# Fetching the edges of 128 work items by one indirect read of 1 KB rows, in the counting stage of a graph network kernel

## The reference, cut to what matters

```
# block 1, three times
h   = x * out_norm[:, None]
agg = segment_sum(h[src], dst, 12500) * in_norm[:, None]
x   = elu(agg @ W + b)
# then x = layernorm(x_in + x)
# block 2, once
msg = relu(x[src] + edge_attr @ W_edge.T + b_edge)
h   = x + segment_sum(msg, dst, 12500)
out = layernorm(x + relu(batchnorm(h @ W1.T + b1)) @ W2.T + b2)
```

## Time and profile before

| | |
|---|---|
| runs | 5515.8, 5519.86, 5517.15 us, median 5517.15 |
| profiled execution | 5517.41 us, its span 5515.5 us |
| counting stage in the span | 0 to about 1724 us |
| busy over the span | PE 91%, DVE 79%, POOL 72%, PE weight loads 56%, ACT 43% |
| `item_edges` gathers | 472, 663.7 us busy, mean 1406 ns |

### The profile page before, as it was taken

The page is one execution under the profiler, slowest core; times in us unless marked ns, Lnnn a source line. Parts: engine busy times, 40 slices in busy tenths (PEclk is TensorE's granted clock), DMA queues, the critical chain, the costliest instruction groups (busy, mean ns, idle before and its releaser), DMA issues.

```text
span 5515.5 us, 115543 instructions
## 1 busy us (share of the span) xinstructions
PE 5016.6 (91%) x41545; PEld 3092.8 (56%) x41546; DVE 4375.9 (79%) x14463; ACT 2369.5 (43%) x4260; POOL 3994.8 (72%) x3849
## 2 busy tenths in 40 slices
PE   7999999999878999999999999888888888887887
PEld 5566666667665555555555544455555555554555
DVE  8899988889897656666556632599999999988997
ACT  4888788887742000000000111244444444444444
POOL 6578877778861777777777777777777777777772
PEclk9999999999998999999999999999999999999997
DMA  5533344433323788888998988522222222222221
GB/s 216 192 128 125 110 151 143 152 135 133 114 81 134 275 283 288 265 289 279 275 280 269 286 296 294 177 47 46 47 45 46 43 45 45 44 44 44 45 46 38
DMA packets 463902, 826.70 MB, mean 150 GB/s; under 512 B 187235, under 2 KB 296049, under 8 KB 456625
## 3 DMA queue, kind: packets, MB, share of 16 engines
q1 hardware_dynamic: 330814, 718.16, 38.3%
q0 software_dynamic: 117952, 75.42, 7.0%
q10 hardware_dynamic: 14562, 25.66, 1.7%
HBM read 616.70 MB, written 202.14 MB: 148 GB/s over the span
## 4 chain that ended last, share of the span: by engine, by line
PE 47%; DVE 26%; POOL 13%; issue 8%; ACT 5%; DMA 1%; POOLq 0%; DVEq 0%; SPq 0%; ACTq 0%
PE banks L2574 22%; DVE tmp L1993 7%; PE banks L2486 7%; POOL rows_f L1299 5%; POOL sorted_recs L1264 5%; PE banks L2449 5%; ACT wide L2211 3%; DVE onehot L1980 3%; PE banks L2735 2%; DVE rows_f L2000 2%; DVE rows_f L1965 2%; PE banks L2456 2%; DVE rows_f L1972 2%; POOL sorted_recs L1209 2%; DVE rows_f L1639 2%
## 5 line engine op out<-in xcount | busy, mean ns | idle before, releaser
L1299 POOL DMA_INDIRECT rows_f<-table,src_key x1465 | 1416.7, 967 | 463.9 <-issue 439.4
L1264 POOL DMA_INDIRECT sorted_recs<-onehot,rows x1280 | 1236.5, 966 | 471.0 <-issue 379.2
L2211 ACT ACTIVATE wide<-banks 128x784 fp8e4<-128x784 f32 x1563 | 1208.4, 826 | 317.2 <-PE banks L2486 312.2
L2574 PE MATMUL banks<-wide,rows_f 128*128 128x512 fp8e4 (+1 forms) x4900 | 1120.0, 375 | 9.8 <-DMA wide<-counts 9.6
L1167 POOL DMA_INDIRECT onehot<-edge_runs_dram,rows_f x472 | 663.7, 1406 | 270.7 <-issue 135.4
L2449 PE MATMUL banks<-wide,onehot 128*128 128x392 fp8e4 x3125 | 783.8, 331 | 0.3 <-ACT wide L2211 0.3
L1993 DVE TENSOR_SCALAR tmp<-iota_win,rows 128x512 f16<-128x512 f16 x2450 | 750.7, 376 | 0.0
L2486 PE MATMUL banks<-rows_f 128*128 128x196 f16 (+2 forms) x5011 | 672.6, 257 | 81.9 <-DVE rows_f L1644 44.9
L2486 PEld LDWEIGHTS banks<-rows_f 128*128 128x128 f16 x5011 | 479.5, 152 | 318.3 <-ACT wide L2211 220.5
L2574 PEld LDWEIGHTS banks<-wide,rows_f 128*128 128x128 f16 x4900 | 441.0, 98 | 386.9 <-issue 9.2
L2735 PE MATMUL banks<-tmp,rows_f 128*128 128x512 f16 x2450 | 591.3, 382 | 14.6 <-DVE rows_f L2000 14.6
(11 more groups left out here) (384 smaller groups left out, 8352.7 us busy)
## 6 DMA issues: line engine op xcount, KB each, us to landing
wide<-counts SPq DMA_DIRECT2D x504, 896.0 KB
counts<-wide SPq DMA_DIRECT2D x49, 3136.0 KB
rows_f<-table,src_key POOLq DMA_INDIRECT x1465
sorted_recs<-rows SPq DMA_DIRECT2D x34, 640.0 KB
sorted_recs<-onehot,rows POOLq DMA_INDIRECT x1280
rows_f<-sorted_recs SPq DMA_DIRECT2D x193, 72.0 KB
agg_a<-attr_dram ACTq DMA_DIRECT2D x50, 250.0 KB
agg_b<-attr_dram ACTq DMA_DIRECT2D x50, 250.0 KB
```

The costliest lines, as they stand in the source:

```text
L1264: G.indirect_dma_start(out=sorted_recs[:, :], out_offset=bass.IndirectOffsetOnAxis(ap=keys_of(t, t + 1).bitcast(I32), axis=0), in_=taken[g ...
L1299: G.indirect_dma_start(out=g_rows[:, n % ROW_RING, k, :], out_offset=None, in_=table32[:, :], in_offset=bass.IndirectOffsetOnAxis(ap=src_k ...
L2211: A.activation(win_counts[o.half % 2][:, :, d0:d0 + o.quads * QUAD].rearrange("p b (q c) -> p b q c", c=QUAD), counted, ACT.Copy, scale=UN ...
L2574: last = M(acc_d[m % 2].rearrange("p (h d) -> p h d", h=2)[:, 0:h, :], layer_rows[n][:, block, :], pieces[:, PLACE[k], 0:h, c * HALF:(c + ...
```

## The change

The host now lays out a wider table. Before, a row of `edge_runs` held one run: 16 sources and 16 destinations, 128 B. Now row j of `item_edges_at` holds the eight runs j to j + 7 one behind the other, 1 KB. So one index an item suffices, and `item_edges` issues one gather of 128 rows of 1 KB in place of eight gathers of 128 rows of 128 B. The bytes that arrive in `stage`, and their places, are the same for all items that lie within the edge list. `find_runs` no longer spreads the first run over eight indices (L1395 goes, L1397 writes one column a chunk, not eight), the constant `iota_run` goes, and `unpack` waits for 16 counts a chunk, not 128.

```diff
-        run_idx = spare[:, RUN_AT:RUN_AT + 2 * RUNS_PER_ITEM * CHUNKS].bitcast(I32).rearrange("p (c j) -> p c j", j=RUNS_PER_ITEM)
-        iota_run = sb("iota_run", [P, RUNS_PER_ITEM])
+        run_idx = spare[:, RUN_AT:RUN_AT + 2 * CHUNKS].bitcast(I32)
...
-            G.iota(iota_run[:, :], [[1, RUNS_PER_ITEM]], base=0, channel_multiplier=0, **exact)
...
-                for j in range(RUNS_PER_ITEM):
-                    G.indirect_dma_start(out=stage[:, c % STAGES, j, :], out_offset=None, in_=edge_runs[:, :],
-                                         in_offset=bass.IndirectOffsetOnAxis(ap=run_idx[:, c, j:j + 1], axis=0)).then_inc(s_stage[c % STAGES], 16)
+                G.indirect_dma_start(out=stage[:, c % STAGES, :, :].rearrange("p r n -> p (r n)"), out_offset=None, in_=item_edges_at[:, :],
+                                     in_offset=bass.IndirectOffsetOnAxis(ap=run_idx[:, c:c + 1], axis=0)).then_inc(s_stage[c % STAGES], 16)
...
-                runs = near[:, c, 0:RUNS_PER_ITEM]
-                link(V.tensor_tensor(runs, over_cells(first_col, a, b, RUNS_PER_ITEM),
-                                     iota_run[:, :].rearrange("p (o j) -> p o j", o=1).to_broadcast([P, b - a, RUNS_PER_ITEM]), ALU.add))
-                V.tensor_scalar(run_idx[:, a:b, :], runs, float(PAD_ROW), None, ALU.min).then_inc(s_find, 1)
+                V.tensor_scalar(run_idx[:, a:b], first_col[:, a:b], float(PAD_ROW), None, ALU.min).then_inc(s_find, 1)
...
-                dve.wait_ge(s_stage[c % STAGES], 16 * RUNS_PER_ITEM * (c // STAGES + 1))
+                dve.wait_ge(s_stage[c % STAGES], 16 * (c // STAGES + 1))
...
+    runs = np.pad(np.stack([np.asarray(src).reshape(RUNS, RUN), np.asarray(dst).reshape(RUNS, RUN)], axis=1).reshape(RUNS, 2 * RUN),
+                  ((0, RUNS_PER_ITEM), (0, 0)), constant_values=-1)
...
+        "item_edges_at": np.concatenate([runs[j:j + RUNS + 1] for j in range(RUNS_PER_ITEM)], axis=1),
```

More of the change, by code:

```diff
@@ L462, with gnn_kernel @@
 ROW_RING, REC_RING, ATTR_RING, HOT_RING = 6, 4, 4, 4
-def gnn_kernel(nc, x, src, dst, dst_rows, edge_runs, edge_recs, attr, w_l0, b_l0, w_edge, b_edge, w1, b1, gamma, beta,
+def gnn_kernel(nc, x, src, dst, dst_rows, item_edges_at, edge_recs, attr, w_l0, b_l0, w_edge, b_edge, w1, b1, gamma, beta,
                w2, b2, out):
@@ L2822 @@
         "dst_rows": np.asarray(dst).reshape(TILES, P),
-        "edge_runs": np.pad(np.stack([np.asarray(src).reshape(RUNS, RUN), np.asarray(dst).reshape(RUNS, RUN)], axis=1).reshape(RUNS, 2 * RUN),
-                            ((0, 1), (0, 0)), constant_values=-1),
+        "item_edges_at": np.concatenate([runs[j:j + RUNS + 1] for j in range(RUNS_PER_ITEM)], axis=1),
         "edge_recs": np.concatenate([np.asarray(edge_attr_16), np.asarray(src).view(np.float32).reshape(EDGES, 1),
```

## The result

| | before | changed |
|---|---|---|
| median of the runs | 5517.88 us (5515.8 to 5523.49, 5 runs) | 5499.43 us (5490.01 to 5501.69, 5 runs) |
| profiled execution | 5517.41 us, span 5515.5 us | 5500.09 us, span 5498.2 us |
| GpSimd busy over the span | 72% | 62% |
| the edge gathers | 472, 663.7 us, mean 1406 ns | 59, 63.7 us, mean 1080 ns |
| VectorE's waits for edges | 18.9 us, once | none |

The changed kernel takes 0.9961 of the time before, 95% interval 0.9946 to 0.9975. That is 18.5 us less, against 20.6 us forecast. Nine tenths of the gathers' GpSimd time are gone, 600 us of 663.7, and 3% of these show in the kernel's time.

The account below looks back on a forecast made before the run. VectorE was taken as the bound from 1300 to 1646 us, with GpSimd falling behind until the ring's slack was gone. Terms -18.9 - 1.7 + 0 = -20.6 us took 5517.4 us to 5496.8 us; range 5489 to 5507 us.

Parts of the forecast that it names:

- The view that was trusted: Counting stage: VectorE's single 18.9 us wait for edges was believed, not the gathers' 79 us share of the chain.
- The hole: VectorE's one stop for edges, before the unpack at 1457.48 us, should close wholly: -18.9 us, bounds -16.9 and -18.9.
- The partial closing: Rival, chance 0.08: VectorE gets its edges but then waits for a free lot buffer, as TensorE is busy; 5507 us.
- The search: VectorE's preparation in `find_runs` gets shorter; four sets inside the stream of lots give -1.7 us, bounds 0 and -2.4.
- The moved constants: GpSimd's constants come up to 17 us earlier at the start; taken as 0, bounds -1.3 to +2 us.
- The early tables: `early_tables` moves from 125 us to about 107 us, behind `find_runs`, where VectorE's lead is gone; 0 to 0.7 us.
- The new gather: Price of the wide gather on GpSimd: 0.94 us, 1.72 us beside lots; no effect on the time.
- The dear gather: Rival, chance 0.03: the wide gather's cost grows faster than its bytes, making GpSimd later; at 18 us, 5535 us.
- The backlog with nine DMAs a chunk: Near 1410 us GpSimd would owe 18.2 us at worst per 17.1 us chunk, against a ring of four chunks.
- A quieter neighbour: VectorE starts a lot every 2.02 us whether GpSimd gathers or is idle, so fewer gathers give it 0.
- VectorE speeding up too: Rival, chance 0.04: each removed gather frees VectorE by 0.15 us, 20 us more where it is the bound; 5477 us.
- The rest: Earlier record writes, GpSimd's longer wait for TensorE behind its last gather, and later stages of unchanged length: worth nothing.

Follow-up runs that it names:

- the late tables: Changed kernel with GpSimd's early IOTAs and MEMSETs issued one set later, behind the gathers of chunks 4 and 5; 5494.6 us, 0.9955 of before.
- the old search: Kernel before with the one wide gather a chunk, but `find_runs` untouched, still writing all eight run numbers; 5496.89 us, 0.9956 of before.
- nine gathers: Kernel before with a ninth gather a chunk, of 64 B rows into a tile nobody reads; 5528.32 us, 1.0017 of before.
- The spread writes: Kernel before, eight gathers kept, late rounds of record writes given one to a chunk instead of packed; 5498.22 us, 0.9964 of before.

## Why the prediction was right

*The view that was trusted.* The chain gave the gathers 30.3% of the stretch from 1200 to 1460 us, 79 us; the waits gave 18.9 us. The waits were right. Seven eighths of the gathers, half of them, or none with the writes moved bring the same.

*The hole, -18.9 us.* Measured -19.00 and -18.99 us. It closed wholly, and nothing came in its place: TensorE took 128.00 us of the 138 ahead of it and VectorE still never waits for it there. The partial closing (0.08) did not happen.

*The search, -1.7 us.* Mis-sized. Forecast 0.42 us a set for four sets; three sets measured 0.30 to 0.42 us, the fourth, at 102 us, 0.42 us in its own instructions (from the addition ahead of the removed one to the lot behind them it is 103.08 to 103.80 us before, 102.16 to 102.46 us now) and then nothing, since the place behind it lost more. The whole is near -1.5 us, and beside the clock at 106 us it does not show in a time at all.

*The moved constants, 0 (bounds -1.3 to +2).* Each size within its bound but for TensorE's clock, the sum a little on the dear side. The 2.50 us IOTA moved to 36.89 us, where VectorE waits for TensorE, as said. That it costs nothing is a matter of place: the kernel with seven gathers moved it by 1 us and paid 3.7 us at its first unpack, more than the forecast's upper bound for all moves. VectorE's first lot came down as said, from 3.23 us to 2.05 us, and chunk 0 to 1 is 1.0 to 1.2 us shorter; the start of chunk 0 is 0.3 us later. The early tables did meet a VectorE without a lead: its first columns behind the search took

```profile
103.06 2.80 DVE L1643 TENSOR_SCALAR rows_f<-rows_f,tmp 128x392 f16<-128x392 f16 x8
```

2.80 us against 2.23 us for the same instruction before, at 104.40 us, which is inside 0 to 0.7; with the late tables it took 2.24 us. What the forecast had not seen is the second step, TensorE's clock, another 1.4 us. Together with 0.6 us between chunks 2 and 4, which I did not follow up (the kernels with the late tables, with the old search and, at 0.5 us, with four gathers have it too, those with seven, eight and nine gathers don't), the moves cost 0.27 - 1.22 + 1.04 + 0.42 + 0.62 = +1.1 us, the 0.42 us being the search's own gain in that stretch.

*The new gather, 0.* 0.94 to 0.98 us at its cheapest, mean 1080 ns, 1.18 us beside the lots of the dense stretch and not 1.72, the price there of many narrow gathers. The dear gather (0.03) is refuted.

*The backlog with nine DMAs a chunk.* The forecast had 18.2 us at worst. From 1260 to 1355 us a chunk takes GpSimd 19.2 us, 3.5 us of them waiting for its slot. What it overlooked are the sixteen writes behind chunk 45: 32.7 us from that chunk's gather to the next. They did no harm, since the gather for chunk 46 was still done 49.9 us ahead of its unpack.

*A quieter neighbour, 0.* Between 537 and 1421 us GpSimd now issues 32 gathers and not 232, and chunk 13 to 45 takes 0.25 us less in one execution and 1.10 us more in the other. VectorE's lots still follow each other in 2.02 us (1381.89 to 1383.91 us in the changed kernel). VectorE speeding up too (0.04) is refuted. Of the exclusive lock of the Trainium skill's page "SBUF - State Buffer", section "SBUF: two separate sides", the gathers show GpSimd's side alone; only GpSimd's IOTAs and MEMSETs are seen to stop VectorE. The 1.10 us are a clock again, at another place: from 828 to 858 us the changed kernel was granted 0.89, in its second execution 1.00, and that stretch alone is 1.3 us longer:

```profile
828.00:858.00 30.00, 27.70 (x279) 0.89 0.41 144
```

```profile
828.00:858.00 30.00, 26.71 (x290) 1.00 0.43 144
```

*The rest.* GpSimd's later wait for TensorE grew from 52.8 to 66.6 us, for nothing, as said.

*The sum.* Forecast -20.6 us; measured -17.3 and -20.7 us between the spans of profiled executions, -18.5 and -23.0 us between medians of two comparisons. At the last unpack it is -18.7 and -19.9 us: the moves cost 1.1 us and the search gave 0.2 us less than forecast, chunk 46 to 58 gave 0.5 us, and chunk 13 to 45 added 1.10 us in the one and took 0.25 us in the other. The later stages then differ by +1.4 and -0.8 us. So that the median fell within 2.1 us of the forecast is in part luck; the hole, nine tenths of the sum, is not.

*What the prediction had not asked.* It took the hole as a matter of the gathers, since they are what the change removes. The spread writes show that it is a matter of the backlog: sixteen DMAs a chunk owed in 17.1 us (24 for chunk 46), of which it is all the same which go. The version with late tables is the fastest of all medians, 5494.6 us, by less than the runs tell from the changed kernel; its trace says 2.3 us.

## What to carry to other kernels

An engine that works ahead into a ring costs nothing until its backlog eats the ring, so price its work by the one wait that it causes (here 18.9 us of 663.7 us of gathers), and ask first whether moving other work off its queue in the dense stretch closes that wait as well. When you size a backlog, take the rate that the late engine has while the others wait for it (1.25 us a DMA here, not the 1.8 us of the 80 DMAs from 1260.6 to 1404.6 us). And where an edit shifts small instructions beside a bound engine, look at the granted clock before you believe an account that is off by one or two microseconds.

## What the hardware did that I had not expected

- **The price of an indirect read by GpSimd did not depend on the bytes of a row** from 64 B to 1 KB: 0.94 us at the cheapest for rows of 64 B, 128 B, 256 B, 512 B and 1 KB, and 0.30 us to the next; 1.04 us for 128 B and for 1 KB at the same place beside VectorE's lots (at 1078 us).
- **TensorE's clock** went to 1.2 GHz behind a wait of 1.88 and 1.89 us in the two executions of the changed kernel and behind 1.75 us with nine gathers, and stayed at 2.4 GHz behind 1.75 us (the kernel before) and behind 2.08 us (the old search). It took 1.4 us, more than the 1.0 us that the edit of the search gave in its three visible sets.
- **A GpSimd IOTA of 2.50 us stopped VectorE** for a CAST of 3.60 us in place of 0.17 us. One gather more or less ahead of it on GpSimd's queue decided whether that lay on the path (3.7 us) or not.
- **A whole chip at 7.5 ms in place of 5.5 ms** for the same program, with DMAs at 181 GB/s in place of 281, and there engines that stop for 10 us and more with nothing in the trace that releases them. With half the gathers the stops from 900 to 1300 us became few and short, those at the start stayed, and 3.2% of the time went. Why is open.
